# Removing filler matmuls, placing the attention tail at the end of its group, and computing the expert gates once

## The reference

```python
x = x + linear_attention(layernorm(x))          # 16 heads of 64, phi = elu+1
y = layernorm(x)
h = y + mla(rmsnorm(y) * g1)                     # causal softmax attention, 16 heads of 64
z = rmsnorm(h) * g2
logits = z @ gate_w                              # 8 experts
top_v, top_i = top_k(logits, 2)
gates = softmax(top_v)                           # the rest of the 8 are 0
ye = silu(z @ w1[e]) @ w2[e]                     # for each expert e, ED = 2048
x = x + (h + sum_e gates[e] * ye)
```

## Time and profile before

| | |
|---|---|
| runs of the kernel before | 3625.81, 3621.07, 3623.39 and 3979.6 us, median 3624.6 |
| profiled execution | 3604.97 us |
| its span on the slowest core (core 6) | 3603.1 us (cores 3579.0 to 3603.1) |
| busy: PE, DVE, ACT, POOL | 2805.6 (78%), 846.0 (23%), 724.4 (20%), 364.7 (10%) us |
| mean granted TensorE clock, core 6 | 0.884 |
| chain that ended last, by engine | PE 67%, DVE 15%, ACT 6%, issue 5%, DMA 5% |
| PE busy in tenths, 40 slices of 90 us | 2778654885464664666999999999999999999997 |
| clock in tenths, the same slices | 9889776895666676877999999999999999999999 |

### The profile page before, as it was taken

How to read it: one execution, slowest core, us unless ns; L and a number is a source line. 1 busy time by engine, 2 the same in 40 slices (tenths; PEclk the granted TensorE clock), 3 DMA queues, 4 the chain that set the end, 5 groups by cost and what they waited for, 6 DMA issues and landing times.

```text
span 3603.1 us, 37958 instructions; the slowest of 8 cores (3579.0 to 3603.1 us)
## 1 busy us (share of the span) xinstructions
PE 2805.6 (78%) x14332; PEld 1261.0 (35%) x14332; DVE 846.0 (23%) x1735; ACT 724.4 (20%) x824; POOL 364.7 (10%) x375
## 2 busy tenths in 40 slices
PE   2778654885464664666999999999999999999997
PEld 1333322432222222223444434444444344344433
DVE  4225444365433223222110010001000100010001
ACT  2002100113252552642011101110111011101110
POOL 0114000000101001002011101110111011101110
PEclk9889776895666676877999999999999999999999
DMA  8001003010000000007256344642563536525641
GB/s 178 1 1 25 1 1 47 1 24 1 1 1 1 1 1 1 1 1 91 24 61 70 33 66 43 71 56 24 62 71 35 71 36 70 59 24 59 71 77 52
DMA packets 297857, 136.02 MB, mean 38 GB/s; under 512 B 268880, under 2 KB 269904, under 8 KB 297680
## 3 DMA queue, kind: packets, MB, share of 16 engines
q0 software_dynamic: 292432, 116.69, 28.3%
q1 hardware_dynamic: 5248, 16.91, 1.5%
HBM read 241.73 MB, written 8.39 MB: 69 GB/s over the span
## 4 chain that ended last, share of the span: by engine, by line
PE 67%; DVE 15%; ACT 6%; issue 5%; DMA 5%; DVEq 1%; another core or an unknown queue 0%; ACTq 0%; POOL 0%; SPq 0%; POOLq 0%
PE PS L986 24%; PE PSQ L958 23%; ACT PTb L758 5%; PE PSQ L293 4%; PE PSQ L747 3%; DVE PTb L768 3%; DMA WSb<-w 3%; DVE accT L996 2%; PE PSQ L404 2%; PE PS L730 2%; PE PST L207 2%; PE PS L813 2%; PE PSQ L359 2%; PE PSQ L564 2%; DMA accT<-x 1%
## 5 line engine op out<-in xcount | busy, mean ns | idle before, releaser
L958 PE MATMUL PSQ<-N,WSb 128*128 128x512 bf16 x4096 | 898.7, 382 | 32.8 <-DMA WSb<-w 29.3
L986 PE MATMUL PS<-N 128*128 128x512 bf16 x2816 | 628.4, 379 | 60.4 <-DVE accT L996 60.4
L996 DVE SCALAR_TENSOR_TENSOR accT<-PS,gts,accT 128x512 f32<-128x512 f32 x256 | 192.1, 751 | 1733.9 <-PE PS L986 1720.5
L958 PEld LDWEIGHTS PSQ<-N,WSb 128*128 128x128 bf16 x4096 | 402.7, 98 | 526.0 <-issue 51.3
L967 ACT ACTIVATE N<-PSQ 128x1024 bf16<-128x1024 f32 x256 | 261.9, 1023 | 1594.2 <-PE PSQ L958 1594.2
L986 PEld LDWEIGHTS PS<-N 128*128 128x128 bf16 x2816 | 270.4, 98 | 409.0 <-issue 92.9
L758 ACT ACTIVATE PTb<-PSQ 128x1024 bf16<-128x1024 f32 x320 | 327.4, 1023 | 238.3 <-PE PSQ L747 222.6
L156 POOL DMA_DIRECT2D WSb<-w x256 | 223.8, 875 | 1210.9 <-PE PSQ L958 1207.8
L986 PE MATMUL PS<-A,N 128*128 128x512 bf16 x1280 | 289.2, 379 | 36.4 <-DVE accT L996 36.4
L730 PE MATMUL PS<-N,PTb 128*128 128x65 bf16 x2176 | 148.5, 219 | 214.0 <-DVE PTb L768 158.2
L747 PE MATMUL PSQ<-qpad,N 128*128 128x512 bf16 x640 | 265.9, 530 | 9.7 <-DVE qpad L692 9.7
(11 more groups left out here) (130 smaller groups left out, 1284.7 us busy)
## 6 DMA issues: line engine op xcount, KB each, us to landing
WSb<-w POOLq DMA_DIRECT2D x256, 256.0 KB, 4.8
N<-w POOLq DMA_DIRECT2D x11, 2048.0 KB, 15.1
A<-w POOLq DMA_DIRECT2D x5, 2048.0 KB, 14.3
accT<-x SPq DMA_DIRECT2D x4, 2048.0 KB, 33.8
out<-accT SPq DMA_DIRECT2D x2, 4096.0 KB, 12.8
N<-aWk POOLq DMA_DIRECT2D x1, 2048.0 KB, 34.7
N<-aWv POOLq DMA_DIRECT2D x1, 2048.0 KB, 56.0
A<-aWq POOLq DMA_DIRECT2D x1, 2048.0 KB, 67.3
```

What stands on the lines that cost most here:

```text
L958: st=(kc == 0), sp=(kc == KD - 1): e_.matmul(out=QB[bb], lhsT=w1slot[sl][:, kk * 128:(kk + 1) * 128], rhs=N1v[:, kk, g * 1024 + hf * 512:g ...
L986: st=(kh == 0), sp=(kh == KH - 1): e_.matmul(out=YEB[pp][:, 0:512], lhsT=N2a[:, kk * 1024 + t_ * 128:kk * 1024 + t_ * 128 + 128], rhs=w2a[ ...
L996: tst = b.emit("v", lambda e_, pp=pair[half], d=dstp, tt_=qt, ee=e: e_.scalar_tensor_tensor(out=d, in0=YEB[pp][:, 0:512], scalar=gts.ap()[ ...
```

## The change

Four things are edited.

1. `keepwarm` and its calls are gone: 4 matmuls behind 15 tiles of the first stage and 3 behind 64 groups of A4, 252 in all.
2. The tail of a group is emitted at the end of its group, and each head's evacuation behind the head. The copies of the next group's first two query blocks (`emit_qpad_copy`) stay ahead of the tail.
3. The multiplication by 1/1024 (L839) goes into the scale of ACT's square root.
4. The logits go to banks 4 and 5 in turn, and DVE only copies them out, one instruction a tile. The gates of all 16 tiles are computed in one batch after the last tail, in ten DVE instructions and one ACT sigmoid of the difference of the two largest logits (in place of an exponential and a reciprocal).

```diff
-            keepwarm(4)
...
-            keepwarm(3)
...
-            if pending_tails is not None and h < 2:
-                deferred_evacs.append((h, par, bkav, pav, tav))
...
-            emit_av_evac(qg, h, bkav, pav, tav)
+            b.wait("v", tav)
...             (the body of emit_av_evac, in place)
...
-                b.emit("v", lambda e: e.tensor_add(out=st[:, 0:1], in0=st[:, 0:1], in1=st[:, 1:2]))
-                tms = b.emit("v", lambda e: e.tensor_scalar_mul(out=st[:, 0:1], in0=st[:, 0:1], scalar1=1.0 / 1024), inc="v")
+            tms = b.emit("v", lambda e: e.tensor_add(out=st[:, 0:1], in0=st[:, 0:1], in1=st[:, 1:2]), inc="v")
-                tsd = b.emit("s", lambda e: e.activation(out=st[:, 2:3], in_=st[:, 0:1], func=AF.Sqrt, bias=EPS_RMS), inc="s")
+            tsd = b.emit("s", lambda e: e.activation(out=st[:, 2:3], in_=st[:, 0:1], func=AF.Sqrt,
+                                                     bias=EPS_RMS, scale=1.0 / 1024), inc="s")
...
-                b.wait("t", bank_free[7])
+            bklg = 4 + (qj % 2)
+            b.wait("t", bank_free[bklg])
...
-                        out=S7[:, 0:8], lhsT=N1v[:, kk, tt * 128:(tt + 1) * 128],
+                    out=SB[pb][:, 0:8], lhsT=N1v[:, kk, tt * 128:(tt + 1) * 128],
...             (the ten DVE steps and the exponential of a tile, removed)
+            tstash = b.emit("v", lambda e, tt=qt, pb=qj % 2: e.tensor_copy(
+                out=gts.ap()[:, tt * 8:(tt + 1) * 8], in_=SB[pb][:, 0:8]), inc="v")
+            bank_free[bklg] = tstash
...
-        if qg == 3:
-            if pending_tails is not None:
-                pending_tails()
-            make_tails()
-        else:
-            pending_tails = make_tails
...
+    b.wait("v", tok_accg[0])
+    b.emit("v", lambda e: e.reduce_max(out=mx3, in_=LG3, axis=AX.X))
...             (four more DVE steps)
+    tsg = b.emit("s", lambda e: e.activation(out=sgc[:, 304:320], in_=sgc[:, 288:304],
+                                             func=AF.Sigmoid), inc="s")
...             (five more DVE steps, the last writes gts)
```

More of the change, by code:

```diff
@@ L126, in build @@
     bank_free = [None] * 8
[L128 to L131, removed]
     def mk_memsets(aps_vals):
@@ L667, in mslot_ap @@
                 else stg2.ap()[:, (qt % 4 - 2) * 1024:(qt % 4 - 2) * 1024 + 1024])
[L669 to L686, removed]
     def emit_qpad_copy(h, qg):
@@ new lines, in build @@
+        tail_toks = []
+        tail_guard = []
+        st = stats.ap()
+        mla_ev = []
+        for qj in range(4):
+            ms = mslot_ap(qg * 4 + qj)
+            ev, _ = transpose_tile(ms, ms.rearrange("p (k n) -> p k n", n=128), av_evac_toks)
+            mla_ev.append(ev)
+        ztoks = []
+        for qj in range(4):
+            qt = qg * 4 + qj
+            ms = mslot_ap(qt)
+            ms_r = ms.rearrange("p (k n) -> p k n", n=128)
+            acc_t = accT.ap()[:, qt * 1024:(qt + 1) * 1024]
+            y_done = []
+            for half in range(2):
+                b.waits("t", [mla_ev[qj], tok_wo2])
@@ L882, in make_tails @@
[L882 to L893 removed]
+                    tw = b.emit("t", lambda e, kk=k, hf=half, mr=ms_r, st_=(k == 0), sp=(k == KD - 1): e.matmul(
+                        out=S7, lhsT=mr[:, kk, :],
+                        rhs=A4r[:, kk, hf * 512:(hf + 1) * 512], start=st_, stop=sp),
+                        inc="t" if k == KD - 1 else None) or tw
@@ new lines, in build @@
+                b.wait("v", tw)
+                b.wait("v", tok_accg[0])
+                b.emit("v", lambda e, a=acc_t, hf=half, tt=qt: e.tensor_scalar(
+                    out=scrF.ap()[:, hf * 512:(hf + 1) * 512], in0=a[:, hf * 512:(hf + 1) * 512],
+                    scalar1=stats.ap()[:, 16 + tt:17 + tt], scalar2=stats.ap()[:, 32 + tt:33 + tt],
+                    op0=ALU.subtract, op1=ALU.mult))
+                ty1 = b.emit("v", lambda e, hf=half: e.tensor_add(
+                    out=scrF.ap()[:, hf * 512:(hf + 1) * 512], in0=S7[:, 0:512],
+                    in1=scrF.ap()[:, hf * 512:(hf + 1) * 512]), inc="v")
@@ new lines, in build @@
+                bank_free[7] = ty1
+                y_done.append(ty1)
+                b.wait("g", ty1)
+                tok_accg[0] = b.emit("g", lambda e, a=acc_t, hf=half: e.tensor_add(
+                    out=a[:, hf * 512:(hf + 1) * 512], in0=a[:, hf * 512:(hf + 1) * 512],
+                    in1=scrF.ap()[:, hf * 512:(hf + 1) * 512]), inc="g")
+            for half in range(2):
+                b.waits("s", y_done)
+                tsq = b.emit("s", lambda e, hf=half, m_=ms: e.activation(
+                    out=m_[:, 0:512], in_=scrF.ap()[:, hf * 512:(hf + 1) * 512], func=AF.Square,
+                    accum_out=st[:, hf:hf + 1]), inc="s")
+                b.wait("v", tsq)
@@ new lines, in build @@
+            ztoks.append(tzt)
+        for qj in range(4):
+            qt = qg * 4 + qj
+            ms = mslot_ap(qt)
+            zev, zmm = transpose_tile(ms, N1v[:, 0:8, qt * 128:(qt + 1) * 128], [ztoks[qj]])
+            tail_toks.append(zev)
+            tail_guard.append(zev)
+            bklg = 4 + (qj % 2)
+            b.waits("t", [zev, tok_gw])
+            b.wait("t", bank_free[bklg])
+            tlg = None
+            for k in range(KD):
+                tlg = b.emit("t", lambda e, kk=k, tt=qt, pb=qj % 2, st_=(k == 0), sp=(k == KD - 1): e.matmul(
+                    out=SB[pb][:, 0:8], lhsT=N1v[:, kk, tt * 128:(tt + 1) * 128],
+                    rhs=gwb.ap()[:, kk * 8:(kk + 1) * 8], start=st_, stop=sp),
+                    inc="t" if k == KD - 1 else None) or tlg
+            b.wait("v", tlg)
+            tstash = b.emit("v", lambda e, tt=qt, pb=qj % 2: e.tensor_copy(
+                out=gts.ap()[:, tt * 8:(tt + 1) * 8], in_=SB[pb][:, 0:8]), inc="v")
+            bank_free[bklg] = tstash
+            tail_toks.append(tstash)
```

152 lines of the change are left out of this document (51 added, 101 removed).

## The result

Seven runs of the changed kernel have a median of 3581.05 us; ten of the kernel before, on the same chips, 3623.61. The ratio is 0.988, with a 95% interval from 0.9854 to 0.9905: 43 us faster (34 to 53). The prediction said 3587, or 37.5 us faster, in a range of 3569 to 3606. (Most of the kernels here also have executions in which the cores of a die ran at a lower granted clock and the time was longer, above 3740 us for the two kernels above; every ratio leaves them out, and so do the medians given further down.)

The account below looks back on a forecast made before the run. Experts were PE-bound; gains had to come from PE's turns with DVE and ACT, worst in the tails' gate chains. 27.0 + 10.3 + 1.5 - 3.8 + 3.2 - 0.7 = 37.5 us, giving 3587, range 3569 to 3606.

Parts of the forecast that it names:

- The gates: Tails of groups 0 to 2: from first logits to next head 6.97 us in place of 15.96, 27.0 saved in three.
- Backlog: Groups 1 to 3: head behind a tail no longer waits for DVE's last gate chain and deferred evacuations; 10.3 us saved.
- table loads: ACT's load back to the exponential moves to head 0's first exponential, where PE waits: 1.28 three times, -3.8 us.
- End of a group: After a group's last product PE idles 1.56 us in place of 2.05; 0.49 three times, 1.5 saved.
- L839: Tails: one of two small steps between ACT's sum and root goes, 0.27 us for each of 12 tiles, 3.2 saved.
- Group 3: Last tail and experts' start: PE starts some 13 us earlier but then waits for panel 4; net -0.7 us.
- panel 4: Expert 0's w1 load queued behind 4 MB of w2: PE waits about 11 us; rival that it is not late, 12 in 100.
- The 0.4 us of slack: Experts' start, kernel before: panel 4 landed at 1680.7 and PE wanted it at 1681.1.
- The restart: Experts, behind the wait at panel 4: the array comes out cold, costing 1.96 us.
- Batched gates: Experts' start: ten DVE steps and a sigmoid with its table load run beside PE's work; taken at 0, uncovered 5 us.
- The fillers: First stage and A4: all 252 lie in front of waits that remain, so removing them gains and costs 0.
- the rival's 22: A4 projection: fillers held the clock, up to 22 us lost without them, gain 15 to 25; 10 in 100.

Follow-up runs that it names:

- the last experiment: Changed kernel with expert 0's first four w1 panels and w2 issued ahead of group 3's tail, other experts' w2 in pieces between panels; ratio 0.976 to the kernel before.

## Why the prediction was right, step by step

- **The gates: right.** 27.0 forecast. From the first logits to the next head the three tails took 47.7 us in all and take 21.1: 26.6. The kernel with this part alone agrees: 26.6 there too and, in its heads and tails, 3.3 and 1.1, in all 31, which is what its ratio gives.
- **Backlog and table loads: right in kind, both too large.** With the end of a group, 10.3 + 1.5 - 3.8 = 8.0 was forecast. All heads together, which hold these three, went from 579.6 to 574.2, 5.4. The kernel with only the tails moved takes them apart: its heads take 7.0 less, 1.5 of it at the ends of groups, so the backlog was worth 5.5 (6.6 by the excess of the three heads alone) and not 10.3. The step that was too large is the one that took the whole excess of the head for backlog; 0.8 to 1.3 a head stays even with the tails in their own place. The changed kernel's heads then take 1.6 more than that kernel's, with three table loads now on PE's path, where 3.8 was put. That is a difference of two profiles and rough. The head behind the tail is still 1.5, 1.6 and 1.5 longer than the next one, the load and PE's slow start (1.87 for four matmuls at 941.05) together. The Trainium skill's 2.66 for a switch (ScalarE: Activation LUTs, What ACT_TABLE_LOAD costs) would by itself be more than the whole excess: ACT's load begins at 942.20 and its exponential at 943.50, with nothing between, so the row decides for 1.3.
- **End of a group: right.** 1.56 against 2.05, three times.
- **L839: the size is not shown by itself.** 3.2 forecast for 12 tiles, 16 x 0.27 = 4.3 with group 3. The tails, from first transposes to first logits, shortened by 5.3. But that is a net: on the six cores with complete records PE's idle time before the output projection fell from 75.4 to 67.3, and its matmuls took 94.1 for 91.3. The kernel whose only edit is the tails' place moved the same stretch by 3.6. So 4.3 fits, and no run here separates it from the clock.
- **The whole stretch ahead of the experts.** From attention's first scores to the first w1 issue 844.8 us before and 807.7 now, 37.1 saved. The terms that lie there come to 27.0 + 10.3 + 1.5 - 3.8 + 3.2 + 0.8 = 39.0.
- **Group 3: right in kind.** PE starts the experts 12 us earlier against the loads (11.3 behind the first w1 issue in place of 23.6) and gets nothing for it: panel 4's matmuls start 40.6 us after that issue, where it was 39.6 and 39.2 was forecast. The wait is 13.2 on the mean, where some 11 was forecast, since panel 4 landed 40.4 after that issue and not 39. The 0.4 us of slack that the prediction read was good for that one profile: in the two kernels that leave this start as it was, the one without fillers and the one with the tails moved, the panel lands 40.6 and 39.1 after the first issue, and six and three of the eight cores wait for it, 0.6 to 4.0 us. The restart was 1.96 forecast: the 192 matmuls behind the wait took 42.88 to 44.05 on six cores with complete records, mean 43.4, against 41.60 where the clock stayed up, 1.8.
- **Batched gates: nothing, right.** On core 6 of the last experiment the chain runs beside PE's first panels:

```profile
1615.23 0.28 DVE L898 TENSOR_REDUCE scrF<-gts 128x16 f32<-128x128 f32 x1
...
1617.12 1.28 ACT L907 ACT_TABLE_LOAD   x1 [12.06 <-DVE scrF L904]
...
1620.62 0.29 DVE L918 TENSOR_TENSOR gts<-scrF 128x128 f32<-128x128 f32 x1
1621.18 1.28 ACT L959 ACT_TABLE_LOAD   x1 [2.55 <-PE PSQ L950]
```

  5.7 us from the first step to the last, ended before ACT's first Silu and long before DVE's first sum. Its second load puts nothing on PE.
- **The fillers: nothing, right.** The measured 1.0014, at most 16 us slower, and the projection's 86.7 leave no room for the rival's 22. The rule that gaps in PE's work let the array drop to half clock (the Trainium skill, TensorE: Matmul & The Clock Gate, HAM oscillation — how this bites in real kernels) is not against this: the clock in A4 is 0.71 with the fillers and without, so it drops either way, and they did not prevent it.

Where is the rest of the 43 us? The traces show 37.1 up to the loads, less 1.0 at panel 4: 36.1. The profiled pair then loses again, at its start (first scores at 792.9 before and 794.6 after) and in the later experts (PE waits for w1 there of 23.1 and 27.6 on the mean of the cores, panel 4 left out). Neither is a cost of the change. The three kernels that share these parts with the kernel before, or lack only its fillers, have their first scores at 795.1 to 795.4 and wait 24.6 to 27.6 in the later experts, so the profiled execution of the kernel before was a quick one in both places. The runs agree: as a mean over the cores, those that enter the ratios took 3599.6 and 3596.5 us in two later rounds of the kernel before and 3560.4 in the changed kernel, 36 to 39 us less, on chips that need not be the same. The 43 is of the slowest core, with an interval of 34 to 53 that holds both. That 37.5 came so near to it owes something to luck: the heads gave 2.6 less than forecast and panel 4 took 1.4 more, the tails gave more than L839's share, and the forecast, made of one core's rows, is nearer to the mean of the cores than to the slowest one that was timed.

## What to carry to other kernels

A chain of tiny steps between two matrix operations costs its full length once per tile, even when every engine looks idle: take it out of the loop, leave one copy, and batch it where a long stretch of PE work covers it. Work that is put off to a later place leaves a queue on the engine that does it, and the bill comes at the next buffer that waits there. When a start gets earlier, ask at once what was loaded just in time for the old one: a small load behind a large one on the same queue cost 13 us here, and cutting the large loads in pieces and starting them earlier brought as much again as the change itself. And a slack of a few tenths that one core of one profile shows is no slack: look at other executions first.

## What the runs showed of the hardware

- A load of 256 KB that is issued behind two of 2 MB on one queue took 25.8 us to land, and moving the large ones only moved the wait (21.5 us). It landed 1.4 to 3.1 us after the second of them on all eight cores, and as close behind it in the profile of the kernel before (1.4 to 1.7), where it was issued some 12 us later.
- The changed kernel's PE waits for w1 are 27.6 to 58.9 us in all, depending on the core, and the spans of its profile differ by 52 us (28.5 to 39 in its other runs that enter the ratio); with small pieces and early loads the waits are 4.1 to 6.4 and the spans within 9 to 25, 12.5 in the profile. So a good part of the unevenness of the cores was in those queued loads.
- Behind the wait at panel 4 (10.5 to 16.3 us) 192 matmuls took 42.88 to 44.05 us, against 41.60 at their shortest: a long wait costs one to two and a half microseconds beside itself. Behind waits of 1.8 to 7.8 in the same profile they took 41.60 in about half of the cases and 43.1 to 44.4 in the others, with 43.29 behind a wait of 2.05 and 41.60 behind one of 3.81, so the length of the wait alone doesn't order them.
- 4 MB of output on one queue and panels of 256 KB on another met: PE stood 4.1 to 6.4 us for a panel.
